# Weighted values ahead of the next batch's first scores, and scaled outputs ahead of the maxima, in three attention phases

## The chip, the cores and the metric

The kernel runs on one core of one Trainium2 chip. The metric is the device time of one execution in microseconds (us). The program is written directly against the engines: each engine has its own instruction stream in program order, and semaphores tie the streams together.

## The reference

The input x is 64 batches of 128 tokens by 128 channels. It goes through six blocks, each followed by a residual sum and a layer norm: a state space scan, a decoder layer with self attention and cross attention, a channel mix, a linear attention, a narrow cross attention and a mixture of experts. The change touches the three softmax attentions only. Cut to them:

```
# self and cross attention (16 heads of 32), inside the decoder layer
q = einsum('bsc,hcd->bhsd', xn, wq); k, v likewise from yn
a = softmax(einsum('bhsd,bhtd->bhst', q, k) * D ** -0.5)
if causal: a = a * mask            # self only, after the softmax
o = einsum('bhst,bhtd->bhsd', a, v)
x_out = x + o @ li1_w + li1_b
# narrow cross attention (16 heads of 8, 77 context rows of 64 channels)
attn = softmax(einsum('bhqd,bhkd->bhqk', qh, kh) * scale)
out = einsum('bhqk,bhkd->bhqd', attn, vh);  return concat(out) @ Wo + bo
```

## The kernel before

The program is a row of phases, one after the other with a barrier between: ssm, self, mlp1, cross, mlp2, mix, gla, narrow, experts. self and cross are the same function, `wide_attention_phase`; narrow is `narrow_attention_phase`. X, XB and XC hold all 64 batches of activations on chip.

An attention phase works on one batch at a time, in a software pipeline. The order is written out by hand: on each engine a loop runs over beats t, and in a beat each engine does its share of several batches at different stages. For one batch n the stages are:

- `first_scores(n)` on PE (L793, narrow L1320): scores with queries as rows, into the four PSUM banks sc[0] to sc[3], one bank for each row group r. In narrow it comes in two halves, banks 0 and 1, then 2 and 3.
- `maxima(n)` on DVE (L1053, narrow L1503): four reductions, one per bank, into nmax. `split(n)` (DVE), `turn(n)` (PE, L803 and L1330) and `turned(n)` (ACT) bring the negated maxima into the row layout nmT.
- `second_scores(n)` on PE (L815 and L819, narrow L1342 and L1346): scores again, with keys as rows and the maxima already taken off, into the same four banks.
- `probabilities(n)` on ACT (L909, narrow L1428): four exponentials out of the banks, into pT. In self, `masked(n)` on POOL multiplies by the mask into pm (L1167).
- `sums(n)` on PE (L829, narrow L1357) adds up each row. `inverse(n)` on ACT makes 1/sum of it (Ln, then Exp, rinv; narrow L1434 and L1436).
- `weighted(n)` on PE (L843, narrow L1369): probabilities times values, into the bank ob. Its waits are for the mask (self) and for `add(n - 1)` having read ob.
- `scaled(n)` on DVE (L1061, narrow L1511): ob times rinv into oT. It waits for weighted(n) and for rinv. `project(n)` on PE (L850, narrow L1375) multiplies by the output weights, again into ob, and `add(n)` on DVE (L1067, narrow L1520) reads it.

There is one set of score banks. So first_scores(t + 1) waits for the exponentials of t - 2, and second_scores of the next beat wait, bank by bank, for the maxima of t + 1:

```
pe.wait_ge(exp_ready, 4 * (n - 2))                       # first_scores
pe.wait_ge(max_ready, 4 * (min(n + 3, N) - 1) + r + 1)   # second_scores, j == 0
```

The second wait stands before the first matmul of bank r, and all four banks come before the fifth matmul group, since PE keeps its order.

In a beat PE does second_scores(t-2), project(t-4), early projection jobs, sums(t-3), first_scores(t+1), weighted(t-3), turn(t), late projection jobs. DVE does split(t), add(t-4), early emptying of projections, statistics and norms, maxima(t+1), scaled(t-3), late emptying. ACT does probabilities(t-2), inverse(t-3), turned(t), its emptying and norms. Batches come in groups of four with one set of projections, so the extra work repeats every four beats. I name a beat by what is done late in it: the beat of x (t % 4 = 0: x, in cross x and context, is turned; earlier in it are the last values), of the queries (1), of the keys (2) and of the values (3). In narrow three beats of four have a projection job before the sums and one has none.

Of the kernel before, what the change touches and what calls it, by code (L numbers as in the profile page):

```python
# [583 lines left out]
def wide_attention_phase(nc, env, name, wd, w, kind):  # L584
# [13 lines left out]
    with Phase(nc, name) as ph:  # L598
# [66 lines left out]
        def there(n):  # L665
            return 0 <= n < N
# [53 lines left out]
        def _(pe):  # L720
# [102 lines left out]
            def sums(n):  # L823
                pe.wait_ge(exp_ready, 4 * n + 4)
                pe.wait_ge(nmT_ready, min(n + 3, N))
                if n:
                    pe.wait_ge(ln_ready, n)
                for r in range(4):
                    mm = pe.matmul(sb[32 * r:32 * r + 32, :], ones[0:TK, :], pT[0:TK, n % 2, r, :])  # L829
                mm.then_inc(sum_mm, 1)  # L830

            def weighted(n):
                s, b = n // GROUP % 2, n % GROUP
                if b == 0:
                    pe.wait_ge(by_dve, (n // GROUP + 1) * N_DVE)
                if own:
                    pe.wait_ge(mask_ready, 4 * n + 4)
                if n:
                    pe.wait_ge(out_read, n)
                for j in range(NT):  # L840
                    for r in range(4):
                        hd = j * P + 32 * r
                        mm = pe.matmul(ob[32 * r:32 * r + 32, j * T:(j + 1) * T], v[0:TK, s, b, hd:hd + 32],  # L843
                                       (pm if own else pT)[0:TK, n % 2, r, j * T:(j + 1) * T])
                mm.then_inc(pv_mm, 1)
# [9 lines left out]
            for t in BEATS:  # L855
                if there(t - 2):
                    second_scores(t - 2)
                if there(t - 4):
                    project(t - 4)
                for g, n in early_jobs(t):  # L860
                    if (g, n) not in FRONT:
                        job(g, n)
                if there(t - 3):
                    sums(t - 3)
                if there(t + 1):
                    first_scores(t + 1)
                if there(t - 3):
                    weighted(t - 3)
                if there(t):
                    turn(t)  # L870
                for g, n in late_jobs(t):
                    job(g, n)
# [93 lines left out]
        def _(dve):  # L966
# [112 lines left out]
            for t in BEATS:  # L1079
                if there(t):  # L1080
                    split(t)
                if there(t - 4):
                    add(t - 4)
                for g, n in early_jobs(t):
                    if (g, n) not in FRONT:
                        empty(g, n)
                norms(t)
                if there(t + 1):
                    maxima(t + 1)
                if there(t - 3):  # L1090
                    scaled(t - 3)
                for g, n in late_jobs(t):
                    empty(g, n)

# [96 lines left out]
def narrow_attention_phase(nc, env, name, wd, w):  # L1191
# [13 lines left out]
    with Phase(nc, name) as ph:  # L1205
# [74 lines left out]
        def _(pe):  # L1280
# [99 lines left out]
            for t in BEATS:  # L1380
                if there(t - 2):
                    second_scores(t - 2)
                if there(t - 4):
                    project(t - 4)
                if g := comes(t, 0):
                    turn_x(g)
                if g := comes(t, 1):
                    queries(g)
                if g := comes(t, 2):
                    context(g)  # L1390
                if there(t - 3):
                    sums(t - 3)
                if there(t + 1):
                    first_scores(t + 1)
                if there(t - 3):
                    weighted(t - 3)
                if there(t):
                    turn(t)

# [61 lines left out]
        @block.vector  # L1461
        def _(dve):
            dve.wait_ge(loaded, 16)
            dve.tensor_copy(bv128[:, :], V("bv").broadcast_to([P, P])).then_inc(setup, 1)
            dve.tensor_copy(pick[:, :, :], bcast(sel, 2, P)).then_inc(setup, 1)
            dve.tensor_copy(ident16[:, :], ident).then_inc(setup, 1)
            dve.memset(nsplit[:, :, :], 0.0).then_inc(setup, 1)
            dve.memset(v[:, :, :, :, :], 0.0).then_inc(setup, 1)
            dve.memset(ones[:, :, :], 0.0).then_inc(setup, 1)
            dve.tensor_scalar(scale_q[:, :], own_head, SCALE, None, ALU.mult).then_inc(setup, 1)  # L1470
            dve.wait_ge(setup, 7)
            for j in range(4):
                last = dve.memset(ones[:, j, D * j:D * j + D], 1.0)
            last.then_inc(setup, 1)
            dve.tensor_scalar(bias_q[:, :], scale_q[:, :], V("bq"), None, ALU.mult).then_inc(setup, 1)
            dve.wait_ge(bias_mm, 1)
            dve.tensor_tensor(bias_o[:, :], pj[1][:, 0:C], V("bor")[:, 0:C], ALU.add).then_inc(setup, 1)
            dve.wait_ge(setup, SET)

            def values(g):  # L1480
                dve.wait_ge(proj_mm, g * NJ + 3)
                dve.wait_ge(by_act, (g + 1) * N_ACT)
                if g >= 2:
                    dve.wait_ge(pv_mm, (g - 1) * GROUP)
                for h in range(2):
                    dve.tensor_copy(v[0:TK, g % 2].rearrange("p b r (j c) -> p (b r) j c", j=4)[:, 8 * h:8 * h + 8, :, 0:D],
                                    pj[h][0:TK, VAL:VAL + 2 * P].rearrange("p (n j d) -> p n j d", j=4, d=D))\
                        .then_inc(v_ready, 1)

            def split(n):  # L1490
                dve.wait_ge(max_ready, 4 * n + 4)
                if n:
                    dve.wait_ge(turn_mm, n)
                dve.tensor_copy(nsplit[:, :, 0:4], nmax[:, :, :]).then_inc(split_ready, 1)
                dve.wait_ge(split_ready, 2 * n + 1)
                dve.tensor_tensor(nsplit[:, :, 4:8], nmax[:, :, :], nsplit[:, :, 0:4], ALU.subtract).then_inc(split_ready, 1)

            def maxima(n):
                if n:
                    dve.wait_ge(split_ready, 2 * n)  # L1500
                for r in range(4):
                    dve.wait_ge(s1_mm, 2 * n + r // 2 + 1)
                    dve.tensor_reduce(nmax[:, r, :], sc[r][:, 0:4 * TK].rearrange("p (h t) -> p h t", h=4),  # L1503
                                      AX.X, ALU.max, negate=True).then_inc(max_ready, 1)

            def scaled(n):
                dve.wait_ge(pv_mm, n + 1)
                dve.wait_ge(rinv_ready, n + 1)
                if n:
                    dve.wait_ge(out_mm, n)  # L1510
                dve.tensor_tensor(oT[:, :], ob[:, 0:T], rinv[:, :], ALU.mult).then_inc(oT_ready, 1)  # L1511

            def add(n):
                g, b = n // GROUP, n % GROUP
                dve.wait_ge(out_mm, n + 1)
                if b == 0:
                    dve.wait_ge(x1b_ready, g + 1)
                    if g >= 2:
                        dve.wait_ge(x_out, g - 1)
                dve.tensor_tensor(y[:, g % 2, b, :], ob[:, 0:C], x1b[:, g % 2, b, :], ALU.add).then_inc(out_read, 1)  # L1520

            def measure(g):
                dve.wait_ge(out_read, (g + 1) * GROUP)
                if g:
                    dve.wait_ge(pool_step, g * 2)
                row_stats(dve, lambda b: y[:, g % 2, b, :], stats[:, :, :], mv[:, :, :], vec, g * VEC, mark)

            def norm(g):
                dve.wait_ge(pool_step, (g + 1) * 2)
                normalise(dve, lambda b: X[:, g * GROUP + b, :], lambda b: y[:, g % 2, b, :], mv[:, :, :], rstd[:, :])\  # L1530
                    .then_inc(x_out, 1)

            values(0)
            for t in BEATS:
                if there(t):
                    split(t)
                if g := comes(t, 3):
                    values(g)
                if there(t - 4):
                    add(t - 4)  # L1540
                if there(t + 1):
                    maxima(t + 1)
                if there(t - 3):
                    scaled(t - 3)
                if t % GROUP == 0 and there(t - 8):
                    measure(t // GROUP - 2)
                if t % GROUP == 1 and there(t - 9):
                    norm(t // GROUP - 2)
# [1491 lines left out]
```

## Time and profile before

| what | us |
|---|---|
| median of 3 runs | 3718.02 |
| lowest and highest | 3712.97, 3718.91 |
| profiled execution, its own time | 3734.92 |
| its span, first to last instruction | 3733.1 |
| self phase, first scores of the first batch to last scaled | about 915 to 1513 |
| cross phase | about 1694 to 2200 |
| narrow phase | about 2980 to 3392 |

The profile is of one execution, which ran 16.9 us (0.45%) over the median. Over the whole span PE is busy 88%, DVE 64%, ACT and POOL 54% each. Matmuls are pipelined and their ends are modelled, so the starts of matmul groups say more than their lengths: the distance between the starts of two groups is what the first one costs PE. A bracket at a row's end is the idle time of that engine just before it, and who ended it.

### The profile page before, as it was taken

Reading aid. Unit: us, or ns where it says so; the run is one execution under the profiler, and the core shown is the slowest. Engines: PE = TensorE matmul, PEld = TensorE weight load, DVE = VectorE, ACT = ScalarE, POOL = GpSimd, SP = SyncE. Lnnn points to the kernel's source line nnn. Section 1 sums busy time; section 2 is a strip of 40 time slices with the busy share of each in tenths; the row PEclk is TensorE's granted clock in tenths of the full one; section 3 lists DMA queues with packets and bytes.
Section 4 is the critical chain, followed back from the end, with each engine's and each line's share of the span. In section 5 each row is a group of like instructions: output and inputs, shape, how many; then the busy total and the mean of one; then the engine's idle time right before and its main releaser. Section 6 shows DMA issues by size and latency. Waiting matters only on the chain. (4 is left out here: it accounts for less than half of the span.)

```text
span 3733.1 us, 102602 instructions
## 1 busy us (share of the span) xinstructions
PE 3290.7 (88%) x41297; PEld 2125.0 (57%) x41297; DVE 2384.4 (64%) x5639; ACT 2008.0 (54%) x3954; POOL 1998.0 (54%) x1774
## 2 busy tenths in 40 slices
PE   7999999996999999878999989968999799996475
PEld 3545455443555555655666667735555467775375
DVE  5888888884455555575555548657777645543365
ACT  5666666662666665434666654336655455563254
POOL 5777787773777787561111126437777501013455
PEclk9999999997999999989999999979999889996698
DMA  4222222226600000000000000000000000000353
GB/s 146 86 82 85 87 90 90 82 82 189 199 2 2 2 2 2 15 10 5 5 5 5 3 6 1 8 7 2 2 2 2 12 16 15 6 5 24 97 167 114
DMA packets 50284, 164.70 MB, mean 44 GB/s; under 512 B 11822, under 2 KB 23217, under 8 KB 40784
## 3 DMA queue, kind: packets, MB, share of 16 engines
q1 hardware_dynamic: 45520, 150.43, 12.4%
q0 software_dynamic: 4352, 8.47, 0.7%
q8 instruction: 296, 4.85, 0.5%
q14 instruction: 116, 0.95, 0.1%
HBM read 149.89 MB, written 43.65 MB: 52 GB/s over the span
## 5 line engine op out<-in xcount | busy, mean ns | idle before, releaser
L496 DVE TENSOR_TENSOR_SCAN XC<-ssm_dA,ssm_db 128x2048 f32<-128x2048 f32 x128 | 565.5, 4418 | 104.6 <-PE ssm_db L352 94.8
L559 POOL TENSOR_TENSOR XC<-XC,XB 128x1536 f32<-128x1536 f32 x128 | 505.9, 3953 | 179.1 <-DVE XC L496 130.0
L366 PE MATMUL ssm_y<-XC,weights 128*128 128x512 f32 x1024 | 471.7, 604 | 2.5 <-POOL XC L559 2.3
L445 ACT ACTIVATE ssm_dA<-ssm_delta,ssm_nega 128x508 f32<-128x508 f32 x512 | 325.1, 707 | 84.5 <-DVE XC L496 84.0
L1167 POOL TENSOR_TENSOR self_pm<-self_pT,weights 128x512 f32<-128x512 f32 x256 | 321.7, 1294 | 58.8 <-ACT self_pT L909 58.8
L366 PEld LDWEIGHTS ssm_y<-XC,weights 128*128 128x128 f32 x1024 | 187.3, 190 | 215.3 <-issue 203.7
L1173 POOL TENSOR_TENSOR XC<-XC,XB 128x128 f32<-128x128 f32 x128 | 59.2, 463 | 400.4 <-DVE XB L1067 400.4
L2384 POOL TENSOR_TENSOR XC<-XC,weights 128x512 f32<-128x512 f32 x128 | 161.8, 1285 | 126.8 <-ACT XC L2221 126.1
L1053 DVE TENSOR_REDUCE self_nmax<-self_scores 128x4 f32<-128x512 f32 x256 | 158.5, 682 | 87.0 <-PE self_scores L793 87.0
L126 POOL TENSOR_SCALAR narrow_rstd<-narrow_mv 128x4 f32<-128x4 f32 x16 | 3.7, 230 | 380.0 <-DVE narrow_mv L121 380.0
L1503 DVE TENSOR_REDUCE narrow_nmax<-narrow_scores 128x4 f32<-128x308 f32 x256 | 105.1, 472 | 156.9 <-PE narrow_scores L1320 156.8
L352 PEld LDWEIGHTS ssm_db<-XB,ssm_dxT 32*128 32x128 f32 x4096 | 134.1, 187 | 99.2 <-DVE XC L496 65.0
L352 PE MATMUL ssm_db<-XB,ssm_dxT 32*128 32x128 f32 x4096 | 159.9, 285 | 25.3 <-DVE XC L496 23.7
L2392 POOL TENSOR_TENSOR XC<-XC,weights 128x512 f32<-128x512 f32 x128 | 161.5, 1284 | 28.8 <-ACT XC L2230 27.5
L909 ACT ACTIVATE self_pT<-self_scores 128x512 f32<-128x512 f32 x256 | 131.7, 599 | 74.8 <-PE self_scores L819 74.8
L909 ACT ACTIVATE cross_pT<-cross_scores 77x512 f32<-77x512 f32 x256 | 131.0, 591 | 69.7 <-PE cross_scores L819 69.5
L1428 ACT ACTIVATE narrow_pT<-narrow_scores 77x512 f32<-77x512 f32 x256 | 131.0, 591 | 68.3 <-PE narrow_scores L1346 68.3
L1653 PEld LDWEIGHTS mlp_yp<-weights,mlp_h 128*128 128x128 f32 x1024 | 133.2, 192 | 58.1 <-issue 56.4
L1681 ACT ACTIVATE mlp_h<-mlp_hp,mlp_bias 128x512 f32<-128x512 f32 x128 | 88.0, 687 | 108.4 <-PE mlp_hp L1645 108.3
L1053 DVE TENSOR_REDUCE cross_nmax<-cross_scores 128x4 f32<-128x308 f32 x256 | 104.0, 467 | 55.9 <-PE cross_scores L793 55.9
L1645 PE MATMUL mlp_hp<-mlp_zT,weights 128*128 128x512 f32 x256 | 133.8, 609 | 1.5 <-ACT mlp_zT L1675 1.5
L1653 PE MATMUL mlp_yp<-weights,mlp_h 128*128 128x128 f32 x1024 | 134.2, 275 | 0.0
(430 smaller groups left out, 8274.0 us busy)
## 6 DMA issues: line engine op xcount, KB each, us to landing
XB<-c_rows SPq DMA_DIRECT2D x64, 1024.0 KB, 4.7
sorted<-in_padding SPq DMA_DIRECT2D x1, 33280.0 KB
experts_we<-in_w_experts SPq DMA_DIRECT2D x72, 323.0 KB, 3.0
experts_rt<-sorted SPq DMA_DIRECT2D x72, 65.0 KB
ssm_xT<-in_xT SPq DMA_DIRECT2D x16, 256.0 KB, 4.7
XC<-in_w_experts SPq DMA_DIRECT2D x9, 256.0 KB
weights<-in_w_self SPq DMA_DIRECT2D x1, 1412.0 KB, 7.4
cross_ctx_t<-in_ctx SPq DMA_DIRECT2D x16, 77.0 KB
```

Source lines behind the costliest of these rows:

```text
L352: mm = pe.matmul(of_batch(db, b)[:, :, 32 * c:32 * c + 32], dxT[rows, slot, half, c, :], diag(slot, c)[rows, nq, :].rearrange("p (k t) -> ...
L366: mm = pe.matmul(yp[half][:, :].rearrange("p (b t) -> p b t", b=GROUP), ident, of_state(states(32, at), k), start=(k == 0 and nq == 0 and ...
L445: o = act.activation(dA[:, p % 2, :].rearrange("p (b k t) -> p b k t", b=GROUP, k=4)[:, :, k, 1:T], by_batch(delta[:, slot, half, :])[:, : ...
L496: dve.tensor_tensor_scan(states(0, p).rearrange("p m t -> p (m t)"), dA[:, p % 2, :], db[:, :], 0.0, ALU.mult, ALU.add).then_inc(h_ready, 1)
L559: pool.tensor_tensor(states(32, p).rearrange("p (b k) t -> p b k t", k=4)[:, :, 0:3, :], states(0, p).rearrange("p (b k) t -> p b k t", k= ...
L909: act.activation(pT[0:TK, n % 2, r, :], sc[r][0:TK, :], ACT.Exp).then_inc(exp_ready, 1)
L1053: dve.tensor_reduce(nmax[:, r, :], sc[r][:, 0:4 * TK].rearrange("p (h t) -> p h t", h=4), AX.X, ALU.max, negate=True).then_inc(max_ready, 1)
L1167: pool.tensor_tensor(pm[:, n % 2, r, :].rearrange("p (h t) -> p h t", h=4), pT[:, n % 2, r, :].rearrange("p (h t) -> p h t", h=4), bcast(V ...
L1645: pe.matmul(hp[j][:, :], w2[:, j * P:(j + 1) * P], zT[:, g % 2, :]).then_inc(h_mm, 1)
L1653: mm = pe.matmul(yp[g % 2][:, b * C:(b + 1) * C], h[:, g % 2, j, b * T:(b + 1) * T], w3[:, j * C:(j + 1) * C], start=(j == 0), stop=(j == 3))
L2384: pool.tensor_tensor(a1(b, r), a1(b, r), bcast(tri, 1, 4), ALU.mult).then_inc(m1_pool, 1)
L2392: pool.tensor_tensor(a2(b, r), a2(b, r), bcast(tri0, 1, 4), ALU.mult).then_inc(m2_pool, 1)
```

## The change

In all three phases PE now runs weighted(t - 3) before first_scores(t + 1), and DVE runs scaled(t - 3) before maxima(t + 1). No instruction is added or removed, and no wait is changed. ACT, POOL and SP have the same instructions in the same order.

```diff
@@ wide_attention_phase, tensor @@
                 if there(t - 3):
                     sums(t - 3)
+                if there(t - 3):
+                    weighted(t - 3)
                 if there(t + 1):
                     first_scores(t + 1)
-                if there(t - 3):
-                    weighted(t - 3)
                 if there(t):
                     turn(t)
@@ wide_attention_phase, vector @@
                 norms(t)
+                if there(t - 3):
+                    scaled(t - 3)
                 if there(t + 1):
                     maxima(t + 1)
-                if there(t - 3):
-                    scaled(t - 3)
                 for g, n in late_jobs(t):
                     empty(g, n)
@@ narrow_attention_phase, tensor: the same exchange as in the first @@
@@ narrow_attention_phase, vector @@
                 if there(t - 4):
                     add(t - 4)
+                if there(t - 3):
+                    scaled(t - 3)
                 if there(t + 1):
                     maxima(t + 1)
-                if there(t - 3):
-                    scaled(t - 3)
```

On PE in the narrow phase, in a beat in which x is turned (L1290), the piece of the difference is this; L1357 are the sums, L1320 the first scores, L1369 the weighted values, L1330 the turn and L1342 the start of the next beat's second scores:

```order
 L1290 MATMUL narrow_proj<-weights,X 128x128 x4
 L1357 MATMUL narrow_sums<-narrow_pT,narrow_ones 32x128 x16
-L1320 MATMUL narrow_scores<-narrow_kT,narrow_qm 128x77 x16
-L1369 MATMUL narrow_out<-narrow_pT,narrow_v 32x128 x16
+L1369 MATMUL narrow_out<-narrow_pT,narrow_v 32x128 x16
+L1320 MATMUL narrow_scores<-narrow_kT,narrow_qm 128x77 x16
 L1330 MATMUL narrow_sums<-narrow_ident,narrow_nsplit 128x128
 L1342 MATMUL narrow_scores<-narrow_nmT,narrow_pick 77x128 x16
```

The sixteen first-score matmuls now stand right in front of the turn and the next beat's second scores; before, the weighted values were between them. It is the same in every beat in which both occur, in all three phases.

On DVE in the cross phase, in the beat of the values, before; L134 are the norms of the input and of the context, L1053 the maxima, L1061 the scaling, L998 the emptying of the values:

```order
 L134 TENSOR_SCALAR cross_xin<-XC,cross_mv,cross_rstd 128x128 x4
 L134 TENSOR_SCALAR cross_ctx_t<-cross_ctx_t,cross_mv,cross_rstd 77x64 x4
 L1053 TENSOR_REDUCE cross_nmax<-cross_scores 128x4 x4
 L1061 TENSOR_TENSOR cross_oT<-cross_out,cross_rinv 128x512
 L998 TENSOR_TENSOR cross_v<-cross_proj,cross_bias_v 77x1024
 L1044 CAST cross_nsplit<-cross_nmax 128x4x4
 L1046 TENSOR_TENSOR cross_nsplit<-cross_nmax,cross_nsplit 128x4x4
```

And the same place after the change:

```order
 L134 TENSOR_SCALAR cross_xin<-XC,cross_mv,cross_rstd 128x128 x4
 L134 TENSOR_SCALAR cross_ctx_t<-cross_ctx_t,cross_mv,cross_rstd 77x64 x4
 L1061 TENSOR_TENSOR cross_oT<-cross_out,cross_rinv 128x512
 L1053 TENSOR_REDUCE cross_nmax<-cross_scores 128x4 x4
 L998 TENSOR_TENSOR cross_v<-cross_proj,cross_bias_v 77x1024
 L1044 CAST cross_nsplit<-cross_nmax 128x4x4
 L1046 TENSOR_TENSOR cross_nsplit<-cross_nmax,cross_nsplit 128x4x4
```

The scaling has moved from behind the four maxima to between the norms and the maxima.

## Rows read from the trace of the kernel before

**Rows 1.** Busy time by engine over the narrow phase (stretch, PE, PEld, DVE, ACT, POOL, clock).
```profile
2980.00:3392.00 412.00, 407.04 (x8143) 291.97 (x8142) 199.75 (x732) 235.13 (x539) 36.65 (x46) 0.96 0.04 11
```

**Rows 2.** Waits of the narrow phase: who waited for whom, total us, times, longest.
```profile
PEld narrow_scores L1320 <- ACT narrow_pT L1428: 8.1, 41, 0.2
```

**Rows 3.** Timeline of PE, one narrow beat: start us, length us, engine, line, operation.
```profile
3175.49 1.08 PE L1357 MATMUL narrow_sums<-narrow_pT,narrow_ones 77*32 77x128 f32 x32
3176.50 1.64 PE L1320 MATMUL narrow_scores<-narrow_kT,narrow_qm 32*128 32x77 f32 x32
3178.06 1.08 PE L1369 MATMUL narrow_out<-narrow_pT,narrow_v 77*32 77x128 f32 x32
3179.08 0.23 PE L1330 MATMUL narrow_sums<-narrow_ident,narrow_nsplit 128*128 128x128 bf16 x1
...
3180.64 0.49 PE L1375 MATMUL narrow_out<-weights,narrow_oT 128*128 128x128 f32 x2
```

**Rows 4.** Timeline of the same narrow beat on ACT and DVE.
```profile
3176.94 0.31 ACT L1436 ACTIVATE narrow_rinv<-narrow_rinv 128x128 f32<-128x128 f32 x1
...
3177.73 1.64 DVE L1503 TENSOR_REDUCE narrow_nmax<-narrow_scores 128x4 f32<-128x308 f32 x4 [2.75 <-PE narrow_scores L1320]
```

**Rows 5.** Timeline of PE, the narrow beat that has no projection.
```profile
3182.07 1.89 PE L1320 MATMUL narrow_scores<-narrow_kT,narrow_qm 32*128 32x77 f32 x32
...
3186.29 0.49 PE L1375 MATMUL narrow_out<-weights,narrow_oT 128*128 128x128 f32 x2
```

**Rows 6.** Timeline of PE, cross phase: beat of the keys, then of x.
```profile
1931.38 1.07 PE L829 MATMUL cross_sums<-cross_pT,cross_ones 77*32 77x512 f32 x8
...
1937.04 1.16 PE L850 MATMUL cross_out<-weights,cross_oT 128*128 128x128 f32 x8
...
1948.01 1.13 PE L793 MATMUL cross_scores<-cross_kT,cross_qT 32*128 32x77 f32 x32
...
1952.24 1.16 PE L850 MATMUL cross_out<-weights,cross_oT 128*128 128x128 f32 x8
```

**Rows 7.** Timeline of DVE, cross phase, beat of the first values.
```profile
1941.08 0.97 DVE L134 TENSOR_SCALAR cross_ctx_t<-cross_ctx_t,cross_mv,cross_rstd 77x64 f32<-77x64 f32 x4
1941.97 1.62 DVE L1053 TENSOR_REDUCE cross_nmax<-cross_scores 128x4 f32<-128x308 f32 x4
1943.51 0.67 DVE L1061 TENSOR_TENSOR cross_oT<-cross_out,cross_rinv 128x512 f32<-128x512 f32 x1
1944.11 1.20 DVE L998 TENSOR_TENSOR cross_v<-cross_proj,cross_bias_v 77x1024 f32<-77x1024 f32 x1
```

**Rows 8.** Timeline of PE, self phase: beats of x, of keys, of values.
```profile
1217.24 1.17 PE L793 MATMUL self_scores<-self_kT,self_qT 32*128 32x128 f32 x32
...
1222.53 1.16 PE L850 MATMUL self_out<-weights,self_oT 128*128 128x128 f32 x8
...
1235.06 1.17 PE L793 MATMUL self_scores<-self_kT,self_qT 32*128 32x128 f32 x32 [0.72 <-ACT self_pT L909]
...
1242.45 1.16 PE L850 MATMUL self_out<-weights,self_oT 128*128 128x128 f32 x8
1243.54 1.06 PE L829 MATMUL self_sums<-self_pT,self_ones 128*32 128x512 f32 x8
...
1250.30 1.16 PE L850 MATMUL self_out<-weights,self_oT 128*128 128x128 f32 x8
```

**Rows 9.** Timeline of DVE, self phase: maxima in the beats of x and keys.
```profile
1218.56 2.48 DVE L1053 TENSOR_REDUCE self_nmax<-self_scores 128x4 f32<-128x512 f32 x4 [0.20 <-PE self_scores L793]
...
1237.49 2.45 DVE L1053 TENSOR_REDUCE self_nmax<-self_scores 128x4 f32<-128x512 f32 x4
```

**Rows 10.** One microsecond each of the narrow phase, columns as in rows 1.
```profile
3035.00:3036.00 1.00, 1.00 (x36) 0.73 (x24) 1.00 (x3) 0.01 (x1) 0.00 (x0) 1.00 0.03 8
...
3037.00:3038.00 1.00, 1.00 (x8) 0.00 (x0) 0.00 (x0) 0.00 (x0) 0.00 (x0) 0.50 0.00 0
```

**Rows 11.** Timeline of PE, narrow phase, at its start.
```profile
3005.37 2.94 PE L1320 MATMUL narrow_scores<-narrow_kT,narrow_qm 32*128 32x77 f32 x32
```

More of the change, by code:

```diff
@@ L1392, in _ @@
                     sums(t - 3)
+                if there(t - 3):
+                    weighted(t - 3)
                 if there(t + 1):
                     first_scores(t + 1)
-                if there(t - 3):
-                    weighted(t - 3)
                 if there(t):
@@ L1540, in _ @@
                     add(t - 4)
+                if there(t - 3):
+                    scaled(t - 3)
                 if there(t + 1):
                     maxima(t + 1)
-                if there(t - 3):
-                    scaled(t - 3)
                 if t % GROUP == 0 and there(t - 8):
```

## Prediction

> **What bounds the kernel now.** I first read the busy times of a phase, then the waits before first_scores, then the timeline of single beats, PE first and DVE beside it. In the narrow phase PE is busy for 407.04 of 412.00 us while DVE has 199.75 and ACT 235.13 [rows 1]. That looks like a phase bound by PE, in which an exchange of two PE steps costs nothing and a filled wait is pure gain. The timeline says otherwise. PE has hardly any wait for the exponentials to fill: 8.1 us in 41 times, 0.2 us each [rows 2]. And there is a second loop that is as long as PE's own work: the score banks. First scores fill them, maxima read them, second scores overwrite them, exponentials read them, and the next first scores may begin.
>
> In the narrow beat shown, first scores start at 3176.50 [rows 3]. The maxima start at 3177.73, 1.23 us later, and last 1.64, to 3179.37 [rows 4]. The next project starts at 3180.64, 1.27 us after that. So **first scores to next project = 1.23 + 1.64 + 1.27 = 4.14 us**, and this is the distance in rows 3. What PE does meanwhile is first scores, weighted values (3178.06 to 3179.08, 1.02 us) and the turn, and it reaches the second scores when the last maximum is just ending. Weighted values are what covers the maxima. Put in front, they cover nothing: first scores start later by them, and PE then waits for the maxima behind.
>
> The same distance in the self phase, in the beat of x: first scores 1217.24, project 1222.53, **5.29 us** [rows 8], with maxima from 1218.56 to 1221.04 and 1.49 us from there to the project [rows 9]. In the cross phase, beat of x: 1948.01 to 1952.24, **4.23 us** [rows 6]. The heavier beats of these two phases (four projections late in the beat) are PE's own, with room behind first scores.
>
> **The change part by part.** Nothing is added or removed, so the sum is made of shifts. Both steps are present in beats 3 to 62, 60 beats in each phase, 15 rounds of four. Weighted values cost PE 1.02 us wherever they stand; sums cost 1.01 (3175.49 to 3176.50) [rows 3].
>
> Their waits don't hold them back in the new place. The add that they wait for follows the project, and between project and weighted values there are at least the sums: in self project 1242.45, sums 1243.54, weighted values at 1244.55 [rows 8]. The mask is from the beat before. On ACT the reciprocal of the narrow beat ends at 3177.25 [rows 4], while weighted values from 3176.50 on would end at about 3177.6, so scaled runs before the maxima can begin (3176.50 + 1.02 + 1.23 = 3178.75). Nobody waits longer for project's input. The matmuls queued behind weighted values are first scores; behind those, DVE's maxima wait.
>
> *Narrow, beats with a projection* (3 of 4). First scores start 1.02 later, the chain is 4.14, so the next project is 1.02 later. Gain from a filled wait: none before the group, since the 0.2 us of rows 2 lies between its halves. 45 beats x 1.02 = 45.9 us.
> *Narrow, beat without a projection.* First scores 3182.07, project 3186.29, 4.22 us, first scores stretched to 1.89 by exponentials that are just ending [rows 5]. After: 3182.07 + 1.02 + 4.14 = 3187.23, 0.94 later. 15 x 0.94 = 14.1. **Narrow: 60.0.**
>
> *Cross, beat of x.* Bound by the chain already, no wait in front: +1.02.
> *Cross, beat of the values.* DVE is last: the norms end at 1942.05 and the maxima start at 1941.97, on their heels [rows 7]. Scaled is now between them. It is 0.67 long and the next instruction starts 0.60 after it [rows 7]: +0.60. The 1.02 of PE's shift is hidden by the norms.
> *Cross, beat of the keys.* Sums 1931.38, weighted values at 1932.39, first scores at 1933.41, + 4.23 = 1937.64; project was at 1937.04 [rows 6]: +0.60. Scaled fits in front of the maxima here, with nothing to spare.
> *Cross, beat of the queries.* Four late projections cover the maxima: 0.
> Sum of a round 2.22, x 15: **cross 33.3.**
>
> *Self, beat of x*: +1.02, as in cross.
> *Self, beat of the values.* Sums 1243.54, weighted 1244.55, first scores 1245.57, + 5.29 = 1250.86, against 1250.30 [rows 8]: +0.56, after the small wait for the exponentials has been filled.
> *Self, beat of the keys.* Here is the gain that the move can have: PE waits 0.72 us for the exponentials before 1235.06 [rows 8]. Filled, all of PE's work behind comes 0.72 earlier, 1242.45 - 0.72 = 1241.73. But the maxima started at 1237.49 behind the statistics [rows 9]; with scaled before them 1238.09, end 1240.54, + 1.49 = 1242.03. The later one counts: -0.42.
> *Self, beat of the queries*: PE's own work is far over the chain: 0, perhaps a tenth gained.
> Sum of a round 1.16, x 15: **self 17.4.**
>
> Together 60.0 + 33.3 + 17.4 = **110.7 us**. The profiled execution took 3734.9, 16.9 over the median; its sum is 3845.6. I put the 110.7 on the median, since the extra 0.45% would change the shift by half a microsecond: 3718.0 + 110.7 = **3829 us, 3.0% slower**.
>
> Two things aren't in the trace and are bounded. One is what follows the maxima after a real wait: at worst the second scores start afresh and the 1.27 us grows by the 0.2 us that a wait of PE shows in rows 2, 12 us over 60 narrow beats; at best the first picks are through by then and it stays 1.27. Rows 8 and 9 show 1.49 behind a wait in self already, so I take no growth. The other is the clock, below.
>
> **The rivals.**
> *Only narrow pays.* For this the heavy phases must absorb their shifts: in self and cross the late projections of one beat would have to make up for the loss in another. For it: the self beats of queries and keys are PE's own. Against it: a beat's delay isn't given back by a later beat unless that one has a wait, and in self only the 0.72 is there. Time: 3718 + 60 = 3778.
> *The clock of TensorE.* With PE busy all the microsecond from 3035 on the granted clock was 1.00, two microseconds later 0.50, 1.2 GHz, again with PE at 1.00 [rows 10]. So the narrow phase has lost the higher clock once with no idle time at all. The change puts about 1 us of idle time into each of its beats. At the low clock first scores last 2.94 us [rows 11] instead of 1.64, 1.30 more; with as much again for second scores a fall costs 2.6, and one in every second beat 30 x 2.6 = 78 more: 3907. Against it: over the whole phase the clock is 0.96 on average [rows 1], and the low stretch at the phase's start, to which rows 11 belong, accounts for most of what is missing. The Trainium skill, page "TensorE: Matmul & The Clock Gate", section "A second HAM failure mode: psum-queue depth-cycling", says that a matmul kernel which went round its PSUM banks idled so often for short moments between groups that the clock went up and down between its two levels. It speaks against this change; by it the time would be the 3907 just worked out, without it 3829, and rows 10 show one fall but no such going up and down.
> *Faster.* The wait for the exponentials is the loss, and filling it is all that happens. This would be so if the second scores had another, later releaser than the maxima. The place is self's beat of keys, the price 0.72 x 15 = 11, with 0.2 in 45 narrow beats another 9: 3718 - 20 = 3698. It decides if after first scores PE still finds 1.02 us of other work beyond the maxima's end in most beats. In narrow it finds only the turn, so this holds in a quarter to a half of the self and cross beats, not where the loss is.
>
> **How the numbers follow.** Forecast, 3829 with its own range of 3800 to 3855 (each phase's sum a fifth off): 0.66. Only narrow pays, 3778: 0.14. Clock, 3907: 0.13. Faster, 3698: 0.05. Nothing measurable, gains and losses cancelling: 0.02. A measurement of this kernel can tell about 0.2%, 7 us. The range of 8 in 10 takes in the forecast's own and the narrow case with some room, 3770 to 3860, and leaves out the clock, the gain and the null, 0.20 together. Faster 0.05, same 0.02, slower 0.93.
>
> **What would show it.** In the profile after, narrow: PE idle by about 1 us in every beat in front of the picks of the second scores (L1342), released by the maxima (L1503), some 60 times; first scores to project still 4.14; the phase 60 us longer and the beat some 7.2 us. DVE: scaled (L1511, L1061) ahead of the maxima without waiting for PE long. Cross: maxima start after scaled right behind the norms; phase 33 longer. Self: the 0.72 wait before first scores gone, waits for maxima up in the beats of x and of values; phase 17 longer. Wrong would be: scaled waiting for the reciprocal and pushing the maxima back (then more than forecast), a clock under 1.00 in the middle of narrow, or a chain shorter than 4.14, which would mean that the second scores don't hang on the last maximum.

## The result: 4.1% slower, 149 us, with the clock as part of it

| | median us | lowest, highest | ratio to before, 95% interval |
|---|---|---|---|
| before | 3716.09 | 3712.97, 3718.91 | |
| changed | 3864.62 | 3858.65, 3873.86 | 1.0411 [1.0390, 1.0432] |

Slower was right. The amount was not: 110.7 us forecast, 148.5 measured, and 3864.6 lies just outside the range that ended at 3860.

The page of the changed kernel's profile shows the same number of instructions, and a lower granted clock in the narrow phase: in the slices wholly inside it (digits 34 to 36 of the row PEclk, which gives the clock in tenths of full speed for 40 equal slices) it reads 988 where the kernel before has 999. Changed, then the same row of before:

```profile
span 3859.8 us, 102602 instructions
PE 3388.5 (88%) x41297; PEld 2206.4 (57%) x41297; DVE 2410.2 (62%) x5639; ACT 2010.1 (52%) x3954; POOL 1998.3 (52%) x1774
...
PEclk9999999997999999979999989989999699887598
```

```profile
PEclk9999999997999999989999999979999889996698
```

**Where it went.** I took the start of each project group from both traces. From the first to the last project of a phase:

| phase | before | changed | difference |
|---|---|---|---|
| self | 558.7 | 579.4 | 20.7 |
| cross | 476.2 | 514.4 | 38.2 |
| narrow | 376.3 | 467.1 | 90.8 |
| sum | | | 149.7 |

The three phases explain the medians. The two profiled spans differ by 126.7 only, mostly because the experts phase at the end, first to last instruction, took 324 us in the profile of before and 300 in that of after. That goes with the chip and not with the code in front: it was 299 to 301 in the four profiles of e5 to e8, which ran on one chip, and 321 to 325 in the seven others of the experiments, which ran on two others.

The distances between neighbouring projects split this further; I call such a distance a beat's length. Nearly all beats of one kind have the same length, and a few are longer, where the clock has fallen. The usual lengths, us:

| beat | before | changed | measured | forecast |
|---|---|---|---|---|
| narrow, x | 6.00 | 6.88 | +0.88 | +1.02 |
| narrow, queries | 6.43 | 7.30 | +0.87 | +1.02 |
| narrow, keys | 6.47 | 7.34 | +0.87 | +1.02 |
| narrow, no projection | 5.65 | 6.44 | +0.79 | +0.94 |
| cross, x | 7.33 | 8.20 | +0.87 | +1.02 |
| cross, queries | 9.41 | 9.14 | -0.27 | 0 |
| cross, keys | 6.74 | 7.24 | +0.50 | +0.60 |
| cross, values | 7.87 | 8.47 | +0.60 | +0.60 |
| self, x | 9.09 | 9.96 | +0.87 | +1.02 |
| self, queries | 9.65 | 9.34 | -0.31 | 0 |
| self, keys | 10.27 | 9.86 | -0.41 | -0.42 |
| self, values | 7.85 | 8.24 | +0.39 | +0.56 |

(A length stands in the row of the beat in which first scores moved.) A round is 3.41 longer in narrow, 1.70 in cross, 0.54 in self; times 15 that is 51.2 + 25.5 + 8.1 = **84.8 us at the full clock**. The other 64.9 us are beats in which the granted clock was low, and the first and last beats of the phases, which the usual lengths don't describe: 39.6 in narrow, 12.7 in cross, 12.6 in self.

**One narrow beat of the changed kernel**, timeline of PE and then of DVE (start us, length us, engine, line, operation), to be held against [rows 3, 4]. It is a beat of x, and rows 3 show one of the keys; the groups shown here are the same in both:

```profile
3257.76 1.08 PE L1357 MATMUL narrow_sums<-narrow_pT,narrow_ones 77*32 77x128 f32 x32
3258.66 1.06 PE L1369 MATMUL narrow_out<-narrow_pT,narrow_v 77*32 77x128 f32 x32
3259.64 1.64 PE L1320 MATMUL narrow_scores<-narrow_kT,narrow_qm 32*128 32x77 f32 x32
3261.21 0.23 PE L1330 MATMUL narrow_sums<-narrow_ident,narrow_nsplit 128*128 128x128 bf16 x1
3261.50 1.48 PE L1342 MATMUL narrow_scores<-narrow_nmT,narrow_pick 32*77 32x128 bf16 x16
3262.77 1.08 PE L1346 MATMUL narrow_scores<-narrow_qm,narrow_kT 32*77 32x512 f32 x8
3263.78 0.49 PE L1375 MATMUL narrow_out<-weights,narrow_oT 128*128 128x128 f32 x2
...
3259.78 0.29 DVE L1511 TENSOR_TENSOR narrow_oT<-narrow_out,narrow_rinv 128x128 f32<-128x128 f32 x1 [2.06 <-PE narrow_out L1369]
3260.88 1.63 DVE L1503 TENSOR_REDUCE narrow_nmax<-narrow_scores 128x4 f32<-128x308 f32 x4 [0.81 <-PE narrow_scores L1320]
```

First scores to project is 3263.78 - 3259.64 = 4.14, to the hundredth what it was in rows 3. The idle time doesn't show as a bracket: the picks, L1342, are stretched over 1.48 us, since each bank's pick waits for its own maximum. In the beat of rows 3 they were

```profile
3179.24 0.60 PE L1342 MATMUL narrow_scores<-narrow_nmT,narrow_pick 32*77 32x128 bf16 x16
3179.62 1.08 PE L1346 MATMUL narrow_scores<-narrow_qm,narrow_kT 32*77 32x512 f32 x8
```

From the picks to what follows them it was 0.38 us and is 1.27 now (3261.50 to 3262.77): PE waits for some 0.9 us in each beat. The last maximum ends at 3262.51. Scaled is 0.29 long and 0.81 us of nothing lie between it and the maxima, so it holds up nobody here.

**The clock.** Granted clock (third number from the right in each row) over five neighbouring stretches of the narrow phase:

```profile
3155.00:3168.00 13.00, 12.83 (x137) 8.53 (x129) 3.36 (x11) 4.05 (x10) 0.00 (x0) 0.50 0.01 3
3168.00:3216.00 48.00, 45.08 (x888) 32.01 (x888) 22.17 (x81) 25.88 (x59) 5.03 (x6) 0.99 0.06 17
3216.00:3229.00 13.00, 12.83 (x148) 8.33 (x137) 3.51 (x12) 3.65 (x9) 0.00 (x0) 0.51 0.01 2
3229.00:3278.00 49.00, 46.07 (x894) 32.61 (x893) 23.02 (x84) 26.28 (x60) 5.05 (x6) 0.99 0.04 11
3278.00:3291.00 13.00, 12.83 (x137) 8.55 (x129) 3.20 (x10) 4.25 (x10) 0.00 (x0) 0.50 0.00 1
```

Six times in the middle of the phase the clock is at its lower level, 1.2 GHz, for 13 to 14 us, and at 2.4 GHz between. The falls come about every 61 us, which is every eighth beat, each time around the beat without a projection. Before, the phase had one short fall [rows 10]. Two more low stretches stand at the phase's start and near its end (17 and 10 us). A fall makes three beats longer, for instance 10.50 instead of 6.44, 7.67 instead of 6.88 and 7.99 instead of 7.34: 5.5 us, six times 33 us.

### The profile page after: what moved, and what is told of

Same layout as the page of the kernel before. It is cut to its first block and busy times, and to the rows that moved or that the text cites. A ratio compares the mean times of both kernels' runs of the same rounds, so it can differ in the third digit from the quotient of the medians.

```text
span 3859.8 us, 102602 instructions
## 1 busy us (share of the span) xinstructions
PE 3388.5 (88%) x41297; PEld 2206.4 (57%) x41297; DVE 2410.2 (62%) x5639; ACT 2010.1 (52%) x3954; POOL 1998.3 (52%) x1774
## 3 DMA queue, kind: packets, MB, share of 16 engines
q0 software_dynamic: 4352, 8.47, 0.6%
## 5 line engine op out<-in xcount | busy, mean ns | idle before, releaser
L1053 DVE TENSOR_REDUCE self_nmax<-self_scores 128x4 f32<-128x512 f32 x256 | 158.7, 682 | 11.3 <-PE self_scores L793 10.6
L1320 PE MATMUL narrow_scores<-narrow_kT,narrow_qm 32*128 32x77 f32 x2048 | 117.9, 300 | 0.6 <-ACT narrow_kT L1420 0.6
```

## The experiments

Ratios are to the kernel before, run beside on the same chip. Its median was 3733.0 for e1 to e4, 3720.2 for e5 to e8 and 3735.5 for e9 to e11, so totals are compared as differences to it.

### e1 and e2: one phase, or the two others

e1 is the narrow function of the changed kernel in the kernel before; e2 the self and cross function of the changed kernel in it.

> Only the narrow phase has both exchanges, self and cross are as before. Theory A (the three phases add up, nothing is passed from one to the next): the narrow phase is some 88 us longer, in falls of the clock by turns (about 33) and beats that are 0.8 to 0.9 us longer at the full clock (3.4 us in a round of four, 51); total 3716 + 88 = 3804. Theory B (the low clock in narrow is a sequel of the changed self and cross phases): the narrow phase is only 51 to 55 longer, total about 3770, and no falls by turns in its middle.

> Only self and cross have both exchanges, narrow is as before. Theory A: self +19, cross +42, total 3716 + 61 = 3777, narrow within 2 us of before. Rival (only the narrow phase pays): total within 0.5% of 3716. By the full-clock beats alone, without the falls of the clock, it would be self +8, cross +26, total 3750.

Measured: e1 3835.4, ratio 1.0262 [1.0214, 1.0311], 102 us over before. e2 3792.0, 1.0157 [1.0140, 1.0174], 59 over. First to last project of narrow is 476.2 in e1 (before 376.3) and 374.9 in e2. First scores of the narrow phase as one group (count, shortest/median/longest ns, first and last start), e1 and then e2:

```profile
L1320 PE MATMUL narrow_scores<-narrow_kT,narrow_qm x2048: 270/270/493, 2983.1 to 3475.6; 32*128 32x77 f32 x187
```

```profile
L1320 PE MATMUL narrow_scores<-narrow_kT,narrow_qm x2048: 270/270/492, 3045.8 to 3436.4; 32*128 32x77 f32 x187
```

492.5 us against 390.6. The phases add up, and narrow's falls of the clock come with the narrow change alone. Theory B is out. In e2, self and cross are 24.0 and 34.7 us longer than before, full-clock beats and a few short falls together. e1 was 14 us over what I expected. In its profile the last fall of narrow is 34 us long and runs to the phase's end; its four executions went from 3808.8 to 3847.5, and only one of them has a trace.

### e3: fill PE's idle time

```diff
             def turn(n):
...
+                for _ in range(8):
+                    pe.matmul(sb[:, 0:T], nsplit[...], ident16[:, :])
                 pe.matmul(sb[:, 0:T], nsplit[...], ident16[:, :]).then_inc(turn_mm, 1)
```

> The changed kernel, with the turn matmul of the narrow phase (bf16, 128 columns) issued nine times in each beat instead of once, the same values into the same place, so that PE works through most of the roughly 1 us in which it waits for the maxima. Theory A (idle time in each beat lets the clock fall): no falls by turns in the middle of narrow, the beats keep their full-clock lengths of 6.88, 7.30, 7.34 and 6.44, narrow some 33 us shorter than in the changed kernel, total about 3830, although PE does more work. Rival (the falls come from something else): the falls stay, total 3865 or more, since each turn adds about 0.1 us to PE.

Measured: 3839.4, 1.0300 [1.0278, 1.0322], 106 over before; the changed kernel, on other chips, was 148.5 and 155 (e10) over. PE timeline (the turns are L1331 and L1332, lines two further down than before from here on), then the granted clock over the phase:

```profile
3301.21 0.62 PE L1331 MATMUL narrow_sums<-narrow_ident,narrow_nsplit 128*128 128x128 bf16 x8
3301.67 0.22 PE L1332 MATMUL narrow_sums<-narrow_ident,narrow_nsplit 128*128 128x128 bf16 x1
3301.82 1.16 PE L1344 MATMUL narrow_scores<-narrow_nmT,narrow_pick 32*77 32x128 bf16 x16
...
3303.78 0.49 PE L1377 MATMUL narrow_out<-weights,narrow_oT 128*128 128x128 f32 x2
```

```profile
3100.00:3200.00 100.00, 96.44 (x1976) 71.43 (x1970) 44.93 (x158) 53.04 (x123) 7.57 (x9) 1.00 0.06 16
3200.00:3300.00 100.00, 96.43 (x1906) 70.11 (x1904) 45.85 (x166) 53.49 (x121) 10.09 (x12) 0.98 0.04 8
3300.00:3400.00 100.00, 96.18 (x1950) 71.07 (x1952) 46.65 (x163) 50.98 (x118) 7.56 (x9) 1.00 0.02 5
```

Eight more matmuls in each beat, and the phase is 41 us shorter than in the changed kernel: 426.0 from first to last project against 467.1. The beats are 6.88, 7.30, 7.34 and 6.44, exactly those of the changed kernel at the full clock; one fall of 3.4 us is left, and the slow start of the phase (11.35 and 8.65 us for the first two beats) is gone too. The eight matmuls take 0.46 us (3301.21 to 3301.67) of the 0.9 that PE waited. The same narrow code took 476.2 in e1 and 476.0 in e10, so the falls cost 41 to 50 us in narrow. By e3 alone it could be the added work and not the filled wait that keeps the clock up; e7 takes the wait away without adding any.

### e7: take the length of the maxima away

```diff
-                    dve.tensor_reduce(nmax[:, r, :], sc[r][:, 0:4 * TK].rearrange("p (h t) -> p h t", h=4),
+                    dve.tensor_reduce(nmax[:, r, :], sc[r][:, 0:4 * TK].rearrange("p (h t) -> p h t", h=4)[:, :, 0:16],
```

The maxima of the narrow phase leave out 61 of 77 keys.

> The changed kernel, with the maxima of the narrow phase taken over the first 16 of the 77 keys of each head only. Theory A (the narrow beat hangs on first scores, maxima, second scores): the maxima are some 0.8 us shorter, the beats come down to PE's own 5.9, 6.3, 6.3 and 5.6, the falls of the clock go, narrow is some 88 us or more shorter than in the changed kernel; total 57 to 61 over before. Rival (the weighted values in front cost PE's time whatever the maxima do): narrow stays 50 or more us over before, total 110 or more over it.

Measured: 3773.7, 1.0139 [1.0124, 1.0153], 53.5 over before. PE and DVE timeline:

```profile
3200.69 1.06 PE L1369 MATMUL narrow_out<-narrow_pT,narrow_v 77*32 77x128 f32 x32
3201.68 1.64 PE L1320 MATMUL narrow_scores<-narrow_kT,narrow_qm 32*128 32x77 f32 x32
3203.25 0.23 PE L1330 MATMUL narrow_sums<-narrow_ident,narrow_nsplit 128*128 128x128 bf16 x1
3203.41 0.78 PE L1342 MATMUL narrow_scores<-narrow_nmT,narrow_pick 32*77 32x128 bf16 x16
...
3204.99 0.49 PE L1375 MATMUL narrow_out<-weights,narrow_oT 128*128 128x128 f32 x2
...
3202.91 0.81 DVE L1503 TENSOR_REDUCE narrow_nmax<-narrow_scores 128x4 f32<-128x64 f32 x4 [0.80 <-PE narrow_scores L1320]
```

With PE's new order untouched, first scores to project went from 4.14 to 3.31 us as the maxima went from 1.63 to 0.81, and the beats to 6.05, 6.47, 6.51 and 5.61, nearly those of before. After the low clock at the phase's start, which here lasted into the first two beats (10.85 and 8.02), there was no fall. First to last project is 381.7, 5.4 over before instead of 90.8: nearly the whole loss of the narrow phase hangs on the maxima being uncovered, and hardly any of it on PE's order by itself.

### e8: half the dose

```diff
                 if there(t - 3):
-                    weighted(t - 3)
+                    weighted(t - 3, 0)
                 if there(t + 1):
                     first_scores(t + 1)
+                if there(t - 3):
+                    weighted(t - 3, 1)
```

This is against the changed kernel; weighted with 0 does j = 0 and 1, with 1 the other two. DVE's order in narrow is that of before; with PE's exchange in place that changes no narrow beat at the full clock (e4 and e11 below have 6.88, 7.30, 7.34 and 6.44 too).

> As the changed kernel in self and cross; in narrow DVE's order of before, and only half of the weighted values (8 of 16 matmuls) in front of first scores, the other half behind. Theory A: first scores are later by half, 0.4 us; beats at full clock 6.4, 6.8, 6.9 and 6.0, 24 us over before in the phase, and no falls of the clock, since half the idle time of PE is gone; total some 85 over before. Rival (it is a question of a gap of any size): falls by turns also here, 110 or more over before.

Measured: 3820.3, 1.0271 [1.0256, 1.0286], 100 over before. The beats are 6.44, 6.86, 6.90 and 6.00, as expected to within 0.06: first scores are 0.43 later, half of 0.87. But the clock did fall, for 3.4 us at a time and twelve times in the phase:

```profile
3200.00:3248.00 48.00, 47.01 (x911) 32.55 (x899) 22.03 (x80) 25.53 (x60) 2.52 (x3) 0.96 0.07 17
3248.00:3251.00 3.00, 2.87 (x23) 1.29 (x24) 1.66 (x12) 0.46 (x1) 1.12 (x2) 0.52 0.00 0
3251.00:3296.00 45.00, 44.02 (x888) 30.98 (x890) 21.06 (x76) 25.96 (x60) 3.90 (x5) 0.99 0.03 6
3296.00:3299.00 3.00, 3.00 (x22) 1.42 (x15) 0.43 (x2) 1.00 (x3) 0.00 (x0) 0.50 0.00 0
```

First to last project is 416.5, 40.2 over before, of which the beats at full clock make 24.8 and the falls most of the rest. Half the idle time still brought falls, shorter and more of them; the no-falls half of theory A was wrong, and the rival, right on the falls, said 110 for what was 100.

### e4, e6, e10 and e11: which of the two exchanges

e4 and e11 are the same kernel, PE's exchange alone; e6 is DVE's alone; e10 is the changed kernel on the chip of e11.

> Only PE's exchange, weighted values before first scores in all three phases; DVE scales behind the maxima as before. Theory A (scaled in front of the maxima costs only where DVE is last): cross values beat 0.6 shorter than in the changed kernel and self keys beat up to 0.3 shorter, 13 us together, narrow the same; total 3851. Rival (the cost is the scaling that stands in front of the maxima): most of the loss goes, total under 3760.

> Only DVE's exchange in all three phases: scaled in front of the maxima, PE in the order of before, so that scaled waits for weighted values that stand behind first scores. Theory A: the maxima wait for 1.0 us of weighted values, the semaphore and 0.6 us of scaling (0.2 in narrow): about 1.0 to 1.3 us in each narrow beat and about 1.7 in the chain-bound beats of self and cross, total 100 to 150 us over before. Rival (DVE has time to spare, 64% busy, so its order costs nothing by itself): within 10 us of before.

> The changed kernel once more, on the chip of the other two runs here, as a reference for the version with PE's exchange alone. By either theory 1.035 to 1.043 of before; self queries, keys and values beats at 9.34, 9.86 and 8.24 and cross values beat at 8.47 at the full clock; narrow with a fall of the clock about every 61 us.

> PE's exchange alone, once more, beside the changed kernel on one chip. Theory A: cross is shorter than in the changed kernel (values beat 7.87 instead of 8.47, 9 us in the phase), self keys beat 9.34 instead of 9.86, but self has more falls of the clock, so that the totals differ by under 25 us. Rival (DVE's exchange takes half of the loss or more): under 75 us over before.

| | median | over before | ratio, 95% interval |
|---|---|---|---|
| e4 PE alone | 3889.0 | 156 | 1.0426 [1.0408, 1.0443] |
| e11 PE alone | 3881.7 | 146 | 1.0380 [1.0349, 1.0411] |
| e10 both | 3890.2 | 155 | 1.0384 [1.0347, 1.0421] |
| e6 DVE alone | 4147.0 | 427 | 1.1113 [1.1073, 1.1153] |

PE's exchange alone costs what both cost. As expected the cross values beat is 7.87 without DVE's exchange (cross 496.8 from first to last project in e11, 508.2 in e10) and the self keys beat 9.34. But self is longer, 595.7 against 581.4, though its beats at the full clock are shorter or the same: there the clock falls in nearly every round without DVE's exchange (75 us at the low level between first and last project, 27 with it). Granted clock over self, e11 and then e10:

```profile
1100.00:1200.00 100.00, 94.63 (x1383) 59.84 (x1382) 55.57 (x141) 58.34 (x113) 77.31 (x85) 0.94 0.01 2
1200.00:1300.00 100.00, 96.42 (x1370) 60.74 (x1366) 48.66 (x127) 59.91 (x116) 70.31 (x73) 0.92 0.01 2
```

```profile
1100.00:1200.00 100.00, 93.78 (x1490) 60.50 (x1488) 56.25 (x139) 59.92 (x117) 78.94 (x87) 1.00 0.01 2
1200.00:1300.00 100.00, 95.17 (x1429) 59.26 (x1431) 55.12 (x138) 63.92 (x124) 77.47 (x83) 1.00 0.01 2
```

Why a difference of half a microsecond in one beat of four decides this wasn't tried. My expectation for e4, 3851, had left these further falls out: it stood for 135 over before, and 156 were measured.

e6 missed by far: 100 to 150 expected, 427 measured, 293 of them in narrow, 70 and 71 in self and cross. DVE waits for weighted values that stand behind first scores, and the low clock then stays. DVE timeline in the narrow phase, the wait of PE's picks, and the clock:

```profile
3445.23 0.29 DVE L1511 TENSOR_TENSOR narrow_oT<-narrow_out,narrow_rinv 128x128 f32<-128x128 f32 x1 [5.72 <-PE narrow_out L1369]
3445.44 1.62 DVE L1503 TENSOR_REDUCE narrow_nmax<-narrow_scores 128x4 f32<-128x308 f32 x4
...
3446.05 1.70 PE L1342 MATMUL narrow_scores<-narrow_nmT,narrow_pick 32*77 32x128 bf16 x16 [0.73 <-DVE narrow_nmax L1503]
```

```profile
3439.00:3446.00 7.00, 6.33 (x100) 4.07 (x99) 1.06 (x4) 5.06 (x11) 2.36 (x3) 0.74 0.01 2
3446.00:3477.00 31.00, 29.22 (x320) 19.14 (x320) 8.26 (x28) 8.38 (x20) 0.00 (x0) 0.51 0.02 4
```

In each 44 us it is low for 34 (once 31 and once 3), over and over; first to last project of narrow takes 669.7 us. So DVE's exchange is dear alone and harmless in narrow beside PE's: with weighted values in front, scaling in front costs DVE nothing there.

### e5 and e9: only where the beats have room

```diff
+                front = t % GROUP in ((1, 2) if own else (1,)) and len(late_jobs(t)) > 0
+                if front and there(t - 3):
+                    weighted(t - 3)
                 if there(t + 1):
                     first_scores(t + 1)
-                if there(t - 3):
+                if not front and there(t - 3):
                     weighted(t - 3)
```

This is e9, PE's exchange in self's beats of queries and keys and cross's beat of queries, nothing on DVE. e5 is the same without the condition on late_jobs.

> The kernel before with PE's exchange alone, and only where the beats of before had room: in self in the beats of queries and keys (t % 4 = 1, 2), in cross in the beat of queries (1). DVE and narrow as before. Theory A (first scores may start later for free where four late projections cover the maxima, and the wait for the exponentials is then filled): self queries beat -0.31, keys beat -0.9, cross queries beat -0.27, 1.5 us in a round, 22 us together, 0.6% faster than before. Rival (each exchange costs its 0.87 us somewhere later): 0 or slower.

> As the picked version, and PE's exchange only where the beat really has late projections, so not in the last three beats of self and cross. The profile of the picked version had the self queries beat at 9.34 (before 9.65), the keys beat at 9.34 (10.27) and the cross queries beat at 9.14 (9.41), 22 us by these, but longer last beats and a fall of the clock there. Theory A: the last beats come back to those of before, 3 to 6 us more gained, total 14 to 17 us under before (0.4%). Rival: the gain at full clock is always eaten at the ends, total 10 under before as in the picked version.

Measured: e5 3710.2, 0.9974 [0.9964, 0.9985], 10 us under before. e9 3723.2, **0.9958 [0.9941, 0.9975]**, 12 us under before, 0.4% faster. PE timeline of e9 in the self beats of queries and of keys:

```profile
1217.64 1.06 PE L829 MATMUL self_sums<-self_pT,self_ones 128*32 128x512 f32 x8
1218.53 1.06 PE L843 MATMUL self_out<-self_pm,self_v 128*32 128x128 f32 x32
1219.51 1.17 PE L793 MATMUL self_scores<-self_kT,self_qT 32*128 32x128 f32 x32
...
1226.98 1.07 PE L829 MATMUL self_sums<-self_pT,self_ones 128*32 128x512 f32 x8
1227.87 1.06 PE L843 MATMUL self_out<-self_pm,self_v 128*32 128x128 f32 x32
1228.85 1.17 PE L793 MATMUL self_scores<-self_kT,self_qT 32*128 32x128 f32 x32
```

The 0.72 us bracket of [rows 8] is gone, both beats are 9.34 (9.65 and 10.27 before) and the cross queries beat 9.14 (9.41): 22.6 us if all 15 rounds had them. First to last project shows 12.2 in self and 2.4 in cross. Part of the rest was never there: before, the keys beat of self had 10.27 in 13 rounds only. Part is lost in single beats of self: two of the early ones took 11.02 and 9.42 instead of 9.34 and 7.85, one of the last 8.94 instead of 7.54. The last has a fall of the clock (3.4 us at 1474). The early ones don't; the clock was 1.00, and PE stood still in the middle of its first scores without any releaser in the trace, for 1.31 us and again for 1.21:

```profile
976.23 0.37 PE L793 MATMUL self_scores<-self_kT,self_qT 32*128 32x128 f32 x1
977.91 1.17 PE L793 MATMUL self_scores<-self_kT,self_qT 32*128 32x128 f32 x31 [1.31 <-issue]
```

```profile
970.00:1000.00 30.00, 27.29 (x410) 16.79 (x411) 15.36 (x44) 18.16 (x36) 21.90 (x23) 1.00 0.83 253
```

Such stops, of 0.5 to 3.7 us, stand between 945 and 995 us in eleven of the thirteen profiles, that of before included. The DMA engines are 83% busy in this stretch (the number before the last of that row); whether that is the cause wasn't tried. e9 is a little faster than both kernels.

## Why the prediction missed, point by point

**What bounds the kernel: right.** The score banks' loop was the bound, and weighted values covered the maxima. e7 shows it for narrow: shorten the maxima and nearly all of the loss is gone. The distance of 4.14 us came back unchanged. The rival "faster" had no ground: its gains, 0.72 in self's keys, did come, but only there and beside the losses.

**The shift of first scores: mis-sized, 0.87 for 1.02.** I took the 1.02 that weighted values cost in front of the turn, and 1.01 for the sums in front of first scores, and assumed that they keep these in another neighbourhood. In the changed kernel the sums cost 0.90 and weighted values 0.98: first scores start 1.88 after the sums instead of 1.01. This is some 0.15 in each beat bound by the loop (0.10 to 0.17 by the table), and it is also half of the -0.31 and -0.27 in the queries beats, for which I had 0. The other half there is a short wait before first scores, now filled: before, they started 1.17 us after the sums in self (1223.62 to 1224.79) and 1.16 in cross, and not 1.0. Forecast at full clock 110.7, measured 84.8.

**Scaling in front of the maxima: right.** +0.60 in the cross values beat, -0.41 for -0.42 in self's keys beat, nothing in narrow.

**The clock: the step that failed.** I named the mechanism, gave it 0.13 and put it at nothing in the sum and outside the range. Low clock and the phases' ends together made 64.9 us. My price of 78 was for narrow alone, as 30 falls of 2.6 us; there it was 39.6, about 33 of it six falls of 5.5 us, and e3 and e7 show that the waits in each beat bring them. For self and cross I had no such term, and 25.3 came. My argument against it was that the clock had stood at 0.96 over the phase with most of what was missing at its start. That was a statement on beats without idle time, and the change was going to add about 1 us of it to every beat; that one fall had come even with PE fully busy [rows 10] spoke for the rival more than 0.13 allows. The Trainium skill, page "TensorE: Matmul & The Clock Gate", section "A second HAM failure mode: psum-queue depth-cycling", describes such a going up and down from short, frequent idle times in a matmul kernel. The traces here agree with it: falls of 13 to 14 us with some 0.9 us of waiting in a beat (e1), twelve of 3.4 us with half of it (e8), one with the wait partly filled (e3), none in the middle with the wait gone (e7). So the outcome has both in it: 84.8 by the forecast's mechanism and 64.9 by what it had left out, 149.7 in all. With only the first, the time would have been about 3803, inside the range.

**Only narrow pays:** this rival didn't come true, as forecast. e2 was 59 us over before.

**What is open.** How many falls a given beat pattern gets. They repeat every eighth beat in narrow, and in self they come in nearly every round without DVE's exchange and seldom with it. How the 64.9 us in all three phases divide into low clock and longer first and last beats wasn't taken apart, and in self and cross nothing was done to the waits to show what brings the falls. For narrow I can say what makes and what removes them, not how many there will be.

## What to carry to other kernels

An engine that the profile shows busy at 99% can at the same time be held by a loop through another one, with nothing to spare: look for a distance between two of its instructions that equals a chain through the other engine, and ask what covers each link before moving the cover. Move filler work in front of a wait only in the iterations in which something else covers the wait behind; here that is 3 of 12 kinds of beat, and it turns 4% slower into 0.4% faster (12 us). If a change adds regular idle time to TensorE, put a price on the clock in the sum itself.

## What the runs showed of the hardware

- A phase with PE 94% busy by the profile (45.08 of the 48 us from 3168 on) lost the higher clock in a repeating pattern once each 6 to 7 us beat had about 0.9 us of waiting in it. Half the wait gave twelve falls of 3.4 us, the full one six of 13 to 14 us, and filling 0.46 us of it with matmuls that compute nothing new left a single one and made the phase 41 to 50 us shorter.
- A group of matmuls costs PE different times in different company, by the distance to the start of the next group. In narrow, sums of 32 columns (77*32) take 0.90 us in front of weighted values of the same shape (77*32), and 1.01 in front of first scores (32*128); weighted values 0.98 in front of first scores and 1.02 in front of the turn. That is 0.15 us a beat from order alone. In self and cross the sums go from 0.99 or 1.00 to 0.88 and the weighted values from 1.01 to 0.98 as well.
- DVE's exchange alone left narrow at the low clock for 514 of 670 us, though PE there is 92% busy by the profile.
